# Copying a projection out of PSUM ahead of the next tile's layer norm, and making the first down-projection weights ternary in two row blocks instead of eight

## What is computed

```python
xn = layernorm(x)
q, k, v = xn @ Wq.T, xn @ Wk.T, xn @ Wv.T          # 16 heads of 128
q = ln_per_head(q * gamma + beta) * 128 ** -0.5
k = ln_per_head(k * gamma + beta)
attn = tril((q @ k.T) ** 2)
o = (attn @ v) / (attn.sum(-1) + 1e-5)
a = o @ Wo.T
y = bit_linear(xn, gate_w)                          # rms norm, 8-bit rows, ternary weights
gate, up = split(y)
f = bit_linear(silu(gate) * up, down_w)             # the same again, 5632 -> 2048
out = x + a + f
```

## Time and profile before

| | us |
|---|---|
| median of 2 runs | 4512.46 |
| the two runs | 4487.46 and 4537.45 |
| profiled execution, device time | 4490.26 |
| its span on the slowest core (core 5) | 4488.7 |
| spans of the 8 cores | 4438.2 to 4488.7 |

### The profile page before, as it was taken

One profiled execution on the slowest core, in us unless ns is written; L12 is line 12 of the kernel. 1 busy time (PEld: TensorE's weight loads), 2 busy tenths in 40 slices (PEclk: granted clock), 3 DMA queues, 4 the chain that ended last, 5 costly groups with the idle time before them and its releaser, 6 DMA issues.

```text
span 4488.7 us, 52826 instructions; the slowest of 8 cores (4438.2 to 4488.7 us)
## 1 busy us (share of the span) xinstructions
PE 2992.9 (67%) x13416; PEld 1270.1 (28%) x13416; DVE 1846.4 (41%) x3416; ACT 1815.6 (40%) x2685; POOL 248.8 (6%) x460
## 2 busy tenths in 40 slices
PE   0776776776776743323268788877888899314888
PEld 0333333333333321111122222223333343112333
DVE  0344453443443433553534322222666665342221
ACT  0333333333333322332256577751444443465551
POOL 1000000000000010000000000000000000000000
PEclk9888887887888876666588899999999999656899
DMA  9434434434434355333221222224677765456885
GB/s 176 119 94 113 122 99 119 111 95 121 114 96 121 113 123 131 103 94 99 75 90 67 91 95 85 81 86 114 231 233 234 235 233 185 159 178 216 280 273 194
DMA packets 326545, 628.24 MB, mean 140 GB/s; under 512 B 199792, under 2 KB 207984, under 8 KB 294256
## 3 DMA queue, kind: packets, MB, share of 16 engines
q0 software_dynamic: 65664, 321.94, 24.5%
q1 hardware_dynamic: 260592, 302.92, 21.6%
HBM read 573.34 MB, written 84.93 MB: 147 GB/s over the span
## 4 chain that ended last, share of the span: by engine, by line
DVE 23%; PE 23%; DMA 17%; ACT 16%; issue 10%; SPq 8%; another core or an unknown queue 3%; DVEq 1%; ACTq 1%; POOL 0%; POOLq 0%
SPq L80 8%; PE kv_ps L357 7%; DMA xf<-xfull 5%; ACT s2t L682 3%; DMA xob<-xown 3%; PE gps L892 3%; PE dps L1118 3%; PE ops L688 2%; DVE kfm L393 2%; ACT sgn L741 2%; ACT sgn L744 2%; PE ups L904 2%; ACT s2t L671 2%; DVE lnst L293 2%
## 5 line engine op out<-in xcount | busy, mean ns | idle before, releaser
L357 PE MATMUL kv_ps<-wk_sb,xnT 128*128 128x512 bf16 x2560 | 646.0, 420 | 199.7 <-DMA wv_sb<-wvt 86.1
L357 PE MATMUL kv_ps<-wv_sb,xnT 128*128 128x512 bf16 x2048 | 476.7, 396 | 98.0 <-DVE kg L367 98.0
L332 PE MATMUL tp_ps<-ident,xnb 128*128 128x128 bf16 x640 | 82.7, 281 | 537.7 <-ACT xnT L338 254.8
L357 PEld LDWEIGHTS kv_ps<-wk_sb,xnT 128*128 128x128 bf16 x2560 | 268.2, 106 | 568.5 <-issue 325.9
L673 DVE TENSOR_TENSOR s2t<-s2t,msk_sb 128x512 bf16<-128x512 bf16 x512 | 217.6, 425 | 415.8 <-ACT s2t L671 409.5
L892 PE MATMUL gps<-terng,xqs 128*128 128x512 bf16 x1408 | 339.6, 397 | 73.2 <-DVE ternu L760 57.3
L688 PE MATMUL ops<-s2t,vsb 128*128 128x512 bf16 x768 | 303.0, 395 | 105.3 <-DVE s2t L673 76.8
L1118 PE MATMUL dps<-dtern,hqts 128*128 128x512 bf16 x1408 | 330.3, 399 | 61.6 <-DMA hqts<-hqtd 61.3
L273 ACT ACTIVATE sgn<-wfp 128x1024 bf16<-128x1024 f32 x264 | 278.9, 1056 | 225.8 <-DMA wfp<-gwt_r 136.8
L671 ACT ACTIVATE s2t<-sps 128x512 bf16<-128x512 f32 x512 | 305.8, 597 | 150.7 <-PE sps L658 121.7
L658 PE MATMUL sps<-qsb,ksb 128*128 128x512 bf16 x768 | 301.1, 396 | 34.4 <-DMA qsb<-qsc 34.4
(11 more groups left out here) (139 smaller groups left out, 3539.3 us busy)
## 6 DMA issues: line engine op xcount, KB each, us to landing
wfp<-gwt_r POOLq DMA_DIRECT2D x176, 512.0 KB, 5.2
wfpt<-gwt_r POOLq DMA_DIRECT2D x88, 1024.0 KB, 6.3
wfp<-dwt_r POOLq DMA_DIRECT2D x88, 512.0 KB, 4.9
xqs<-xqsc SPq DMA_DIRECT2D x88, 512.0 KB, 4.5
wfpt<-dwt_r POOLq DMA_DIRECT2D x44, 1024.0 KB, 8.3
hqts<-hqtd SPq DMA_DIRECT2D x32, 1408.0 KB, 8.5
xf<-xfull SPq DMA_DIRECT2D x32, 1024.0 KB, 7.6
hgscr<-hgb SPq DMA_DIRECT2D x88, 256.0 KB, 2.6
```

The lines of the kernel that those rows point to most:

```text
L357: TE(lambda e, jj=j, f=fc, w=w_sb: e.matmul(kv_ps[jj][:], xnT[:, f * 128:(f + 1) * 128], w[:, f * DM + jj * 512: f * DM + (jj + 1) * 512], ...
```

## The change

Three edits. First, `featuremap` is cut in two: `featuremap_evac` holds the four multiplies by gamma that read PSUM, `featuremap` the rest. In stage 1 `featuremap_evac(kck)` and the V projection are emitted ahead of `ln_tile` for the next tile, and the rest of `featuremap` behind it. (PE has no instruction in `ln_tile`, so PE's own order stays the same.) Second, in stage 2 `featuremap_evac(qck)` is emitted right behind the Q projection, ahead of the stores of the tile before and of `ln_tile`. Third, in stage 4b a chunk is made ternary after every piece of the row blocks 0 and 1 (22 pieces) instead of after the pieces 0, 4 and 8 of each row block.

```diff
-    def featuremap(dst_bf, q_scale, mm_cks, dst_waits):
+    def featuremap_evac(mm_cks):
         for j in range(4):
             v = V(lambda e, jj=j: e.tensor_tensor(
                 kg[:, jj * 512:(jj + 1) * 512], kv_ps[jj][:],
                 gmb[:, jj * 512:(jj + 1) * 512], ALU.mult),
                 waits=[(cT, mm_cks[j]), (s_misc, ck_misc0)])
             st["kv_evac"][j] = ("cV", v)
+
+    def featuremap(dst_bf, q_scale, dst_waits):
         V(lambda e: e.tensor_add(kg[:], kg[:], btb[:]))
...
+        featuremap_evac(kck)
+        vck_banks = proj_mm(wv_sb, first_waits=[])
+        st["xnT_free"] = cT.n
         if t + 1 < NT:
             st["xn_ck"][t + 1] = ln_tile(xf[(t + 1) % 2], want_f32=False,
                                          xslot=(t + 1) % 2)
-        fm_ck = featuremap(kfm, q_scale=False, mm_cks=kck,
+        fm_ck = featuremap(kfm, q_scale=False,
                            dst_waits=st["kfm_free"])
-        vck_banks = proj_mm(wv_sb, first_waits=[])
         emit_abs(2)
-        st["xnT_free"] = cT.n
...
         st["xnT_free"] = qck[-1]
+        featuremap_evac(qck)
         emit_abs(3)
...
-        fm_ck = featuremap(kfm_ring[slot], q_scale=True, mm_cks=qck,
+        fm_ck = featuremap(kfm_ring[slot], q_scale=True,
                            dst_waits=kfm_free2[slot])
...
-            if jc % 4 == 0:
+            if s < 2:
                 emit_dtern(1, max_m=0)
```

## The result

| | before | after |
|---|---|---|
| median, us | 4505.0 (32 runs) | 4529.6 (33 runs) |
| spans of the 8 cores in the profiled execution, us | 4438.2 to 4488.7 | 4487.6 to 4515.3 |
| mean of the 8 spans | 4464.7 | 4501.8 |

The ratio after to before is 1.0055, with a 95% interval of 1.0035 to 1.0074, so about +25 us. Under 2%, but not nothing. (A program on eight cores has executions in which one die runs at a lower clock; ratios leave these out, the medians hold them.) I had forecast 4498 us, +8 on one profiled execution.

What follows compares the result with a forecast made beforehand. Dependence chains bound it: DVE's in stages 1 and 2, ACT's pace in stage 4b. Terms 39 - 15 - 16 = +8 us on the profiled 4490.3 gave 4498 us, range 4462 to 4540.

Steps and rivals of the forecast that it cites:

- Stage 1, +39 forecast: Stage 1: layer norm queued behind K's end costs 0.97 us in 30 tiles, plus PE idling and first tile: +39 us.
- `xf` is 3.1 us ahead of K's end: Stage 1: next tile's rows land 3.1 us before K's matmuls end; 2.6 would give +24 us, 3.6 would give +54.
- has 50 us to spare: Stage 1, core 0: the edit would cost +1.9 us a tile there, but that core was taken to have 50 us spare.
- Stage 2, -15 forecast: Stage 2: multiplies leave the DVE chain, -22.3 us over tiles 1 to 7, +6.9 in the first tile: -15 us.
- the 6.9 forecast: Stage 2, first tile: the layer norm for tile 1 now comes behind the fourth multiply, +6.9 us.
- Stage 4b, -16 forecast: Stage 4b: 32.6 us of load waits go; 3.4 (fence), 10 (paired chunks) and 3 (borders) come: -16 us.
- One sign of being wrong: Stage 4b: a load taking over 11 us was named as something that would show the forecast wrong.
- some 0.5 us at 6 borders: Stage 4b: two DVE pieces in a row and PE's in-order transposes at each row block border cost +3 us in all.
- the first (PE bounds the tile, 4361): Stage 1: the tile waits for PE, so 98.0 us come back; with stages 2 and 4b 4361 us; chance 0.04.
- The second: Stage 1: the layer norm's delay is hidden, so the stage changes by 0, total 4459 us; chance 0.12.
- the third: Stage 4b: dense loads collide, so the stage gains nothing or loses up to 15 us, 4514 to 4529; chance 0.12.
- The fourth (the clock): Stage 1: PE idles longer behind V and K runs longer at half clock, for example 4603 us; chance 0.05.

Runs made afterwards that it cites:

- the second edit alone: Only the stage 2 edit (multiplies ahead of the stores and the layer norm) against the kernel before: ratio 0.9947 (0.9911 to 0.9983).

## Why the prediction was wrong

**The sign of the sum was right, the number was not.** I added +8 us to a single execution of 4490 and called the result 4498. With 32 runs the kernel before is at 4505, and the change costs 25. Two mistakes lie in it. I put the forecast below the median of the two runs then known (4512), so that as a statement on the measured change it said faster, while my own sum said slower. A change has to be carried onto the number it will be compared with. And two of the three terms were off. By the means of the cores the stages changed by +53, -12 and -6, the whole span by +37 (4464.7 to 4501.8). The slowest core rose by less, 26.6 us in the profiled executions, since it stood 24.0 us above the mean before and 13.5 after. The terms:

- **Stage 1, +39 forecast, +53 on average of the cores.** The mechanism held. L372 was forecast 6.6 us behind K's end and is at 6.62, the layer norm takes 5.57, V 13.98. On core 5 a later tile grew by 1.25 us, 1.02 of them at the add, for 1.12 forecast; the first tile lost 5.2 us for the 5.6 forecast; stage 1 grew by 43.6 us. The step that failed is the sizing on core 5 alone: "`xf` is 3.1 us ahead of K's end", and the sentence that core 0 "has 50 us to spare". On average of the eight cores DVE could start the layer norm 3.5 us ahead of K's end (2.9 to 4.1), so the add stood 5.28 us behind it, not 5.65, and the reordering costs 1.35 us a tile there, not 0.97; that alone is 11 us over 30 tiles. I had seen that core 0's loss per tile would be double (1.9 us, from the earlier trace rows against the earlier trace rows), and set it aside because core 5 was the slowest. But core 5 was among the slow ones in part because its `xf` came late in that execution, and just that made its loss one of the smaller ones. In other executions other cores have that role: in the profile of the second edit alone, for one, stage 1 took 1475 us on core 2, the core that had the longest one, 1502, in the execution I predicted from. After the change every core is at 1540, and which core is last is decided elsewhere. The right term was the mean over the cores, +51 to +53, less what the spread of the cores gives back: the slowest core stood 26 us above the mean in 36 executions of the kernel before, and 17 in 27 of the changed one.
- **Stage 2, -15 forecast.** Measured -12 on average, -16 on core 5. From the last V matmul to the first add it was 102.4 us on core 5 and is 107.2, +4.8 for the 6.9 forecast; on average of the cores 99.4 and 107.0, +7.7. Later adds are 3.5 us closer on core 5 and 3.25 on average, for 3.2.
- **Stage 4b, -16 forecast.** Measured -6. On core 3 the new waits between chunks were much as forecast: ACT waited 11 times for DVE's add, 12.3 us in all, and the one load behind the store cost 4.2 us (3.4 forecast, 5.3 on core 5). All eleven loads stand ahead of the second store, not ten, which changes no number. One sign of being wrong was met by a hair: two loads took 11.2 and 11.4 us on core 5, but nothing waited for them. The term that failed is the border: "some 0.5 us at 6 borders", priced by DVE and PE's order, while the reads of h late behind the store made it 1.5 to 2.4 us each (21.0 to 21.9 us a row block against 19.5 forecast, and 19.2 once six buffers hide them). The rows could have warned: the earlier trace rows shows the load behind that same store at 9.2 us. I used it for the weights and did not ask what else is on those DMA engines at that time. The Trainium skill, "DMA: Bandwidth & Descriptors" (Issuing engines are not separate DMA queues), says that DMAs of all issuing engines interleave on the same 16 engines. The trace agrees as far as it goes: the reads on SP's queue took 4.9 us beside the store on POOL's and 3.0 elsewhere. I weighed it only for the loads of weights, and it was the reads of h that waited.

Of the rivals, the first (PE bounds the tile, 4361) fell as expected: the 98 us went, and PE's wait for `kfm` grew from 31 to 199. The second fell with stage 1, the third with stage 4b, which gained 6 us: what came late there were reads beside the store and not the dense loads of weights. The fourth (the clock) fell too: K at 15.94 us against 15.93 on average of the cores. The Trainium skill, "TensorE: Matmul & The Clock Gate" (Why this matters for your kernels), says that idle gaps between matmul bursts bring the throughput down. The trace of the changed kernel agrees for V: no group stands behind a gap and each takes 13.98 us, off the path, as weighed. But the 1.5 us of one tile were too many for all: before, V took 14.96 us on average on core 5, 17 of 32 groups were slow, and the length of the gap did not say which (15.53 us behind 2.33 us, 13.97 behind 3.61).

What I missed altogether is the better change that the same rows offered. DVE's 395.8 us of waiting for `xf` in the earlier trace rows were read as the thing that sets the tile, and the forecast asked only what the reordering does to it, not why the load comes late.

## What to carry to other kernels

When an instruction group is moved ahead of another on an in-order engine, look at what each waits for. The multiplies wait for K's end, the layer norm for a load that came earlier, and putting the one that is released later in front makes the earlier one as late. A gap that closes on PE (98 us here) is worth nothing when the next thing PE waits for hangs on the other engine. A load that is late for no better reason than its place in a queue is worth moving first (111 us of stage 1, 30 of stage 4b). And with eight cores, size an edit from the mean of the cores, since the slowest core of one profile may be slow for the very wait that the edit touches.

## What the runs showed of the hardware

A load that every core issues behind 32 small stores let the layer norm start 2.9 to 4.1 us ahead of K's end (averages of the cores before), and stage 1 took 1468 to 1509 us in 48 core traces of the same code; released by matmuls instead, 32 core traces lay within 1535 to 1549, and with the load ahead of the stores and the old order the 8 of one execution lay within 1372 to 1381. Reads of 256 KB issued on SP took 4.9 us to land beside a store of 1.4 MB issued on POOL and 3.0 us elsewhere (core 3 of the changed kernel), and ended up to 2.4 us after they were wanted (4.2 on core 6) with three buffers; with six, none of it was left in the length of a row block (19.2 us against 21.0 to 21.9). K took the same time (15.93 and 15.94 us) behind a stretch without projection matmuls of some 14 us as behind one of 19.
